# First expert stage: second product in three rounded parts, first product issued three blocks ahead, and the work beside it in another order

## The reference

```python
def _L0_ffn_ref(x, Wg, W1, W2, W3):                    # E = 8 experts, F = 256, top 2
    scores = jnp.einsum('bsd,ed->bse', x, Wg)
    topk_scores, topk_idx = jax.lax.top_k(scores, 2)
    topk_probs = jax.nn.softmax(topk_scores, axis=-1)
    h1 = jnp.einsum('bsd,efd->bsef', x, W1)
    h2 = jnp.einsum('bsd,efd->bsef', x, W2)
    hidden = jax.nn.silu(h1) * h2
    expert_out = jnp.einsum('bsef,edf->bsed', hidden, W3)
    onehot = jax.nn.one_hot(topk_idx, scores.shape[-1], dtype=x.dtype)
    gating = jnp.einsum('bsk,bske->bse', topk_probs, onehot)
    return jnp.einsum('bse,bsed->bsd', gating, expert_out)
...
    x = _layernorm(x + _L0_attn_ref(x, ...))           # "front" work: output projection, norm, router
    x = _layernorm(x + _L0_ffn_ref(x, ...))            # experts; "back" work: residual, norm
    x = _layernorm(x + _L1_attn_ref(x, ...))           # "back" work also: q, k, v of this attention
    x = _layernorm(x + _L1_ffn_ref(x, ...))
```

## Time and profile before

| | us |
|---|---|
| median of 3 runs (lowest to highest) | 1793.75 (1791.52 to 1801.08) |
| the profiled execution: its time | 1795.82 |
| its span, first to last instruction | 1794.0 |
| first copy of y in the first expert stage to the last | 407.9 to 757.9 |
| TensorE busy, VectorE busy, ScalarE busy over the span | 92%, 80%, 68% |
| mean granted TensorE clock | 0.965 |

### The profile page before, as it was taken

One profiled execution on the slowest core, in us unless ns is written; L12 is line 12 of the kernel. 1 busy time (PEld: TensorE's weight loads), 2 busy tenths in 40 slices (PEclk: granted clock), 3 DMA queues, 4 the chain that ended last, 5 costly groups with the idle time before them and its releaser, 6 DMA issues.

```text
span 1794.0 us, 33595 instructions
## 1 busy us (share of the span) xinstructions
PE 1642.9 (92%) x11168; PEld 846.0 (47%) x11168; DVE 1443.7 (80%) x2519; ACT 1213.3 (68%) x1843; POOL 107.4 (6%) x187
## 2 busy tenths in 40 slices
PE   5899999699999999869999999999999978888887
PEld 3333333266556656524444444444444436665565
DVE  3779999867777777688999999999999926778777
ACT  3889999643444444318888888888888876655555
POOL 1000000001101010210000000000000000001000
PEclk9899999899999999969999999999999988999999
DMA  7572323101101111220111111111111010000000
GB/s 219 152 223 82 98 83 94 51 14 49 36 23 38 48 48 35 96 65 30 42 36 36 36 36 35 41 35 36 36 43 49 21 40 14 20 20 19 26 18 12
DMA packets 63717, 95.92 MB, mean 53 GB/s; under 512 B 22512, under 2 KB 31600, under 8 KB 62976
## 3 DMA queue, kind: packets, MB, share of 16 engines
q1 hardware_dynamic: 63616, 94.56, 17.4%
HBM read 51.01 MB, written 43.52 MB: 53 GB/s over the span
## 4 chain that ended last, share of the span: by engine, by line
PE 70%; DVE 11%; issue 8%; ACT 5%; SPq 3%; DMA 2%; POOL 1%; DVEq 0%; ACTq 0%; POOLq 0%
PE full_o L717 15%; PE hid_pair L1014 11%; PE max_pair L688 11%; PE score L702 7%; PE causal_o L449 5%; PE bank L1103 5%; PE triple L433 5%; PE bank L1023 2%; DVE negmax_h L802 2%; PE bank L1044 2%; PE bank L1115 2%; ACT cprobs L477 1%; ACT o_sb L776 1%; SPq L591 1%; PE bank L1069 1%
## 5 line engine op out<-in xcount | busy, mean ns | idle before, releaser
L802 DVE TENSOR_REDUCE negmax_h<-max_pair 128x2 f32<-128x1024 f32 x512 | 620.8, 1222 | 40.0 <-PE max_pair L688 38.6
L768 ACT ACTIVATE probs<-score 128x512 f32<-128x512 f32 x1024 | 556.0, 597 | 118.8 <-PE score L702 70.6
L717 PE MATMUL full_o<-probs,v_st 128*32 128x256 f32 x4096 | 327.7, 392 | 16.3 <-ACT o_sb L776 16.3
L477 ACT ACTIVATE cprobs<-triple 128x1536 f32<-128x1536 f32 x192 | 265.6, 1454 | 21.2 <-PE triple L433 18.4
L688 PE MATMUL max_pair<-k_st,q_st 64*128 64x512 f32 x1024 | 262.1, 509 | 9.9 <-DVE negmax_h L802 9.8
L702 PE MATMUL score<-q_st,k_st 64*128 64x512 f32 x1024 | 224.5, 405 | 0.3 <-ACT probs L768 0.3
L688 PEld LDWEIGHTS max_pair<-k_st,q_st 64*128 64x128 f32 x1024 | 98.0, 188 | 222.5 <-issue 187.3
L1014 PE MATMUL hid_pair<-x_hi,w_hi 128*128 128x512 f32 x384 | 182.4, 475 | 6.9 <-ACT act_s L1216 6.8
L1211 ACT ACTIVATE act_s<-hid_pair 128x512 f32<-128x512 f32 x128 | 76.4, 597 | 158.3 <-PE hid_pair L1014 158.3
L507 DVE TENSOR_SCALAR cprobs<-cprobs 128x1536 f32<-128x1536 f32 (+6 forms) x272 | 163.4, 624 | 0.4 <-ACT cprobs L477 0.4
L717 PEld LDWEIGHTS full_o<-probs,v_st 128*32 128x32 f32 x4096 | 82.0, 108 | 169.1 <-issue 87.0
(11 more groups left out here) (136 smaller groups left out, 1696.0 us busy)
## 6 DMA issues: line engine op xcount, KB each, us to landing
o_scr<-o_sb SPq DMA_DIRECT2D x64, 256.0 KB, 2.1
k_st<-k_scr SPq DMA_DIRECT2D x64, 128.0 KB, 2.9
q_st<-q_scr SPq DMA_DIRECT2D x128, 64.0 KB, 2.4
q_st<-q_scr SPq DMA_DIRECT2D x16, 512.0 KB
k_st<-k_scr SPq DMA_DIRECT2D x64, 104.0 KB
q_scr<-qk_hi SPq DMA_DIRECT2D x24, 256.0 KB, 2.9
k_scr<-qk_hi SPq DMA_DIRECT2D x24, 256.0 KB, 3.4
q_scr<-qk_lo SPq DMA_DIRECT2D x16, 256.0 KB, 3.0
```

The lines of the kernel that those rows point to most:

```text
L477: nc.scalar.activation(cprobs[n % CP][:, :, :], triple[n % 2][:, :, :], ACT.Exp, scale=SCALE).then_inc(L.exp_done, 1)
L717: last = nc.tensor.matmul(full_o[SLOT * j:SLOT * (j + 1), cols], v_st[p][:, kt, j, :], probs[s % NP][:, j, cols], start=(kt == 0 and part ...
L768: nc.scalar.activation(probs[s % NP][:, L.HEADS[j], :], sbank[L.score_bank(e)][:, :], ACT.Exp, scale=SCALE).then_inc(L.exp_done, 1)
L802: nc.vector.tensor_reduce(negmax_h[:, qt // TPC, half, heads[0]:heads[1] + 1:2, qt % TPC], ring[slot][:, :, :], AXX, ALU.max, negate=True) ...
```

## The change

The second product takes three F32R matmuls. ScalarE rounds `hid` to `hid0_hi` (`act_upper`), VectorE subtracts for `hid0_lo` (`dve_lower`), both three buffers deep, and `w3` is split once ahead of chunk 0. The hidden product goes three blocks ahead, the engines' beside work comes two blocks late, and the plan puts the front ahead of the back. The copy of y moves into block 2 of the next chunk. The `Fori` loops over chunks 1 to 6 are written out, in both layers. Zeroing is cut in eight pieces, GpSimd's work is interleaved by step, and the loads of `x` share four semaphores.

```diff
-LATE = (0, 2)
+LATE = (2, 2)
+HB0 = 3
...
-    BESIDE_BACK = {4: (0, 1), 5: (2, 3), 6: (4, 5)}
+    BESIDE_BACK = {6: (0, 1), 7: (2, 3), 8: (4, 5)}
+    CLEARS = 2
...
+            w3_hi = overlay.enter_context(nc.sbuf_tensor("w3_hi", [P, NH, P], F32R))
+            w3_lo = overlay.enter_context(nc.sbuf_tensor("w3_lo", [P, NH, P], F32R))
...
-        for pl, steps in ((plan[0], (1, 3, 4, 5, 6, 7, 8, 9, 10, 11, None, 12, 13, 14)),
+        for pl, steps in ((plan[0], (2, 4, 6, 7, 8, 9, 1, 1, 3, 4, None, 5, 7, 12)),
...
-        h_banks, h_lead = [2, 3], [1, 3]
+        h_banks, h_lead = [2, 3], [3, 3]
+        w_splits = [3, 5]
...
+        FIRST_ROWS = {SPC - 3: 0, SPC - 1: 1}
+
+        def rows_at(n, layer):
+
+            per = SPC // n_exp[layer]
+            if layer == 0:
+                e = (n + 3) // per if n % per == 1 else E0
+            else:
+                e = n // per if n % per == per - 2 else E1
+            return e if e < n_exp[layer] else None
...
                 if n == pl.x2_turn:
                     pe.wait_ge(st.norm2, back + 1)
+                    if front is not None:
+                        pe.wait_ge(st.gate_pre, front + 1)
                     pe_turn_tiles(bank[2], x_out).then_inc(st.xt2_turned, 1)
...
-            pe.wait_ge(st.hid_ready, c * SPC + n + 1)
-            nc.tensor.matmul(bank[0][:, :], w3[:, n, :], hid[n % 2][:, :], start=(n == 0),
-                             stop=(n == SPC - 1)).then_inc(st.y_done, 1)
+            q = c * SPC + n
+            pe.wait_ge(st.lo_ready, q + 1)
+            hi, lo = hid0_hi[q % HB0], hid0_lo[q % HB0]
+            for a, (w, x) in enumerate(((w3_hi, hi), (w3_lo, hi), (w3_hi, lo))):
+                last = nc.tensor.matmul(bank[0][:, :], w[:, n, :], x[:, :], start=(n == 0 and a == 0),
+                                        stop=(n == SPC - 1 and a == 2))
+            last.then_inc(st.y_done, 1)
...
-            with pe.Fori(0, B - 1) as u:
+            for u in range(B - 1):
...
+        def act_upper(act, st, q):
+
+            act.wait_ge(st.hid_ready, q + 1)
+            wait_used(act, st.y_done, q - HB0 + 1)
+            nc.scalar.activation(hid0_hi[q % HB0][:, :], hid[q % 2][:, :], ACT.Copy).then_inc(st.hi_ready, 1)
...
         def act_chunk(act, st, c, par, back, front, layer):
             for n in range(SPC):
+                if layer == 0 and n == LATE[0] and back is not None:
+                    act_save_y(act, st, back)
                 act.wait_ge(st.h_ready, c * SPC + n + 1)
                 wait_used(act, st.hid_ready, c * SPC + n - 1)
                 if layer == 0:
                     nc.scalar.activation(act_s[n % 2][:, :], hbank[n % 2], ACT.Silu).then_inc(st.s_done, 1)
+                    if c * SPC + n > 0:
+                        act_upper(act, st, c * SPC + n - 1)
...
+                if layer == 0 and n == plan[0].x_turn:
+                    act.wait_ge(w_lower, 2)
+                    nc.scalar.activation(w3_hi[:, :, :], w3[:, :, :], ACT.Copy).then_inc(w_upper, 1)
...
+        def dve_lower(dve, st, q):
+
+            dve.wait_ge(st.hi_ready, q + 1)
+            wait_used(dve, st.y_done, q - HB0 + 1)
+            nc.vector.tensor_tensor(hid0_lo[q % HB0][:, :], hid[q % 2][:, :], hid0_hi[q % HB0][:, :].bitcast(F32),
+                                    ALU.subtract).then_inc(st.lo_ready, 1)
...
                     nc.vector.tensor_tensor(hid[n % 2][:, :], act_s[n % 2][:, :], lin_u[n % 2][:, :],
                                             ALU.mult).then_inc(st.hid_ready, 1)
+                    if c * SPC + n > 0:
+                        dve_lower(dve, st, c * SPC + n - 1)
...
+                if layer == 0 and n == plan[0].g_turn:
+                    dve.wait_ge(w_upper, w_splits[0])
+                    nc.vector.tensor_tensor(w3_lo[:, :, :], w3[:, :, :], w3_hi[:, :, :].bitcast(F32),
+                                            ALU.subtract).then_inc(w_lower, 1)
...
                 if c == 2 * B - 1:
+                    sp_first_full(sp, layers[1])
+                    sp.wait_ge(st.y_done, 2 * B * SPC)
                     sp.dma_start(w_raw[0][:, :], d["we1"]).then_inc(raw_loaded[0], 16)
                     sp.dma_start(w_raw[1][:, :], d["we2"].rearrange("p n c -> p (n c)")).then_inc(raw_loaded[1], 16)
-                    sp_first_full(sp, layers[1])
```

More of the change, by code:

```diff
@@ L311, in build_program @@
             x_out = osb("x_out", [P, TPC, D])
+            hid0_hi = [osb(f"hid0_hi{i}", [P, CH], F32R) for i in range(HB0)]
+            hid0_lo = [osb(f"hid0_lo{i}", [P, CH], F32R) for i in range(HB0)]
         q_scr0 = nc.dram_tensor("q_scr0", [B, P, 2, T], F32, kind="Internal").ap()
@@ L336, in build_program @@
         layers = [Causal(sem), Full(sem)]
+        X_GROUPS = [(0,), (1,), (2, 3), (4, 5, 6, 7)]
+        x_group = [k for k, cs in enumerate(X_GROUPS) for c in cs]
         class Stage:
@@ L352, in __init__ @@
                 if n == 0:
-                    self.x_in = [sem(f"st0_x_in{c}") for c in range(2 * B)]
+                    self.x_in = [sem(f"st0_x_in{k}") for k in range(len(X_GROUPS))]
                     self.pair_stored = [sem(f"st0_pair_stored{p}") for p in range(2)]
@@ L1056, in pe_beside @@
                     if layer == 0 and back is not None:
-                        pe.wait_ge(st.v_saved, back + 1)
+                        wait_used(pe, st.v_saved, back)
                     for t in range(TPC):
@@ L1185, in act_beside @@
                     nc.scalar.activation(gate_t[:, :], bank[3][0:2 * E0, :], ACT.Copy).then_inc(st.gate_t, 1)
-                if n == SPC - 1 and layer == 0:
-                    act_gate_rows(act, st, front, 0, layer)
+                if layer == 0 and n in FIRST_ROWS:
+                    act_gate_rows(act, st, front, FIRST_ROWS[n], layer)
         def act_gate_rows(act, st, c, e, layer):
@@ L1235, in act_end @@
                         nc.scalar.activation(w_hi[k][:, :], w_raw[k][:, :], ACT.Copy).then_inc(w_upper, 1)
+                if layer == 0 and n == plan[0].x_turn:
+                    act.wait_ge(w_lower, 2)
+                    nc.scalar.activation(w3_hi[:, :, :], w3[:, :, :], ACT.Copy).then_inc(w_upper, 1)
             act_chunk(act, st, 0, 0, None, 1, layer)
-            with act.Fori(0, B - 1) as u:
+            for u in range(B - 1):
                 act_chunk(act, st, 2 * u + 1, 1, 2 * u, 2 * u + 2, layer)
@@ L1449, in dve_end @@
             dve_chunk(dve, st, 0, 0, None, 1, layer)
-            with dve.Fori(0, B - 1) as u:
+            for u in range(B - 1):
                 dve_chunk(dve, st, 2 * u + 1, 1, 2 * u, 2 * u + 2, layer)
@@ L1469, in pool_rstd, with pool_beside, pool_end0, pool_end1 @@
             nc.gpsimd.tensor_tensor(rstd[:, k, :], rstd[:, k, :], mhalf[:, :], ALU.pow).then_inc(sig, 1)
-        def pool_back(pool, pc, st, c, layer):
-            pool_rstd(pool, pc, st.stats2, st.rstd2, 1, c + 1)
-            if layer == 0:
-                for a in range(2):
-                    pool.wait_ge(st.rot_done, 2 * c + a + 1)
+        def pool_beside(pool, pc, st, n, back, front):
+            pl = plan[0]
+            if front is not None and n == pl.o_proj:
+                pool_rstd(pool, pc, st.stats, st.rstd, 0, front + 1)
+            if back is not None and n == pl.y_turn:
+                pool_rstd(pool, pc, st.stats2, st.rstd2, 1, back + 1)
+            for a, at in enumerate((pl.q, pl.k)):
+                if back is not None and n == at:
+                    pool.wait_ge(st.rot_done, 2 * back + a + 1)
                     nc.gpsimd.tensor_tensor(rot[2 * a][:, :], rot[2 * a][:, :], rot[2 * a + 1][:, :],
                                             ALU.add).then_inc(st.rot_sum, 1)
-        def pool_end(pool, st, layer):
+        def pool_end0(pool, st):
+            pc = Chain(pool, st.pool_chain)
+            for n in range(SPC):
+                pool_beside(pool, pc, st, n, None, 0)
+            for c in range(2 * B):
+                back, front = c - 1 if c > 0 else None, c + 1 if c < 2 * B - 1 else None
+                for n in range(SPC):
+                    if n >= LATE[0]:
+                        pool_beside(pool, pc, st, n - LATE[0], back, front)
+                    if c == 2 * B - 1 and n >= SPC - 2:
+                        for k in range(layers[1].CLEARS):
+                            pool_clear_full(pool, layers[1], layers[1].CLEARS * (n - SPC + 2) + k)
+            for k in range(2 * layers[1].CLEARS, CPB * HG):
+                pool_clear_full(pool, layers[1], k)
+            for n in range(SPC):
+                pool_beside(pool, pc, st, n, 2 * B - 1, None)
+        def pool_end1(pool, st):
             pc = Chain(pool, st.pool_chain)
```

61 lines of the change are left out of this document (33 added, 28 removed).

## The result

The changed kernel takes 1813.03 us (median of 6 runs, 1810.73 to 1822.06) where the kernel before takes 1793.68 in the same rounds (6 runs): ratio 1.0104, 95% interval 1.0073 to 1.0136. It is slower by 1.0%, about 19 us, against the +7 forecast, and its median lies 1 us above the forecast's range of 1776 to 1812.

The account below looks back on a forecast made before the run. TensorE alone was taken to bound the kernel before, a cycle through TensorE and VectorE the new one. Six chunks +17.4, chunk 0 +1.0, chunk 7 -6.0 and loops -5.4 made +7.0 on 1793.75: 1800.8 us, range 1776 to 1812.

Parts of the forecast that it names:

- The cycle through both engines: Steady first-stage chunks: waits in program order through TensorE and VectorE sum to 53.7 us for 50.8, +17.4 over six.
- The collision with GpSimd: First rotary sum of 1.27 us starting during weigh: VectorE delayed by 0.3, bounds 0 and 1.27.
- Chunk 7: Last chunk of the first expert stage, which has no front: 39.2 us for 45.2, -6.0.
- step 2: VectorE from hid 9 to the end of the second rotary pair: 7.43 us, plus 0.3 for GpSimd's rotary sum.
- The ends: Terms outside the steady chunks: first chunk +1.0 us, last chunk -6.0, loop back edges of the second expert stage -5.4.
- the written-out loops: Second expert stage, chunks 1 to 6: without back edges -5.4 us, bounds 0 and -5.6.
- I take 2.7 twice: Two back edges in the second expert stage, each a 2.78 us VectorE gap, disappear: -5.4 us.
- The third rival: Writing out the chunk loops does nothing, so the -5.4 falls away: 1806 us, chance 0.13.
- the forecast's term for the moved waits: Chunk 0 of the first expert stage: moved rows and waits together give -0.4 us.
- The second rival: GpSimd's rotary sum blocks VectorE's weigh in full, 0.85 us, 0.55 more than taken: 1804 us, chance 0.17.
- The first rival: First-stage plan keeps its covers, VectorE running ahead: 1765 us, or 1778 with half the waits kept; chance 0.22 at 1778.

Follow-up runs that it names:

- the second execution: Unmodified changed kernel run and profiled once more, in the rounds of the fillers experiment: 1812.97 us, ratio 1.0114 against the kernel before.
- loops alone: Kernel before with only the chunk loops of both expert stages written out on TensorE, ScalarE and VectorE: 1789.50 us, ratio 0.9990.
- the best variant: Changed kernel with weigh, x2_turn and y-copy repairs, x_turn and its followers one step later, copy of v on ScalarE: 1784.73 us, ratio 0.9946.

## Why the prediction was wrong

**The mechanism held.** The cycle through both engines, by its own steps, in the chunk shown above:

1. End of top 2 (488.90 + 0.17) to `hid` 9 at 494.00: 4.93 for 4.76. The two loads of 1.28 stand back to back with the exponential between them, as the forecast took them from the earlier trace rows; from the first load to silu (490.50 to 493.31) are 2.81 again. The drain of 1.38 per load of the Trainium skill (ScalarE: Activation LUTs, "What ACT_TABLE_LOAD costs") is not seen here either.
2. `hid` 9 to the end of the second rotary pair (501.49 + 0.68): 8.17 for 7.73. **The collision with GpSimd was sized at 0.3 and is 0.88**: 1.04 for 0.16.
3. From there to the copy of y at 520.91: 18.7 for 18.45.
4. Copy of y (466.85) to `hid` 2 at 468.02: 1.2 for 1.4.
5. `hid` 2 to the end of top 2: 21.05 for 21.4.

Sum 54.1 for 53.7. Moving one edge at a time took 1.4, 1.5 and 1.0 away, for 2.1, 1.3 and 1.4 expected. That the sum is off by only 0.4 is partly luck: the five steps are off by +0.2, +0.4, +0.3, -0.2 and -0.3. Chunk 7 came as worked out, 39.1 for 39.2. The waits stand where the text put them: `ot`, `xs`, `lead`, the rotary results.

**The steps that failed** are terms of the sum that were sized too small or too favourably, nearly all on the same side: GpSimd's collision in step 2, chunk 0 in "The ends", and the written-out loops. By the second execution's +18.7 less 7.0, 11.7 are missing:

- **Up to the first copy of y**: +5.5 for +1.0, the largest of them. 1.4 of it is there before the stage starts (the last `causal_o` at 340.67 for 339.26); this start varies, from 337.1 to 343.2 in the sixteen profiles. The second gate row added 1.48 for the 1.4 forecast. The other 2.7 lie between the first hidden product and the first copy of y, where the forecast had -0.3: about 1.4 of them are the clock and 1.3 the change, as the rows below show.
- **The cycle**: +20.7 for +17.4, of which some 2.4 are GpSimd's collision and the small errors above (54.1 for 53.7) and 0.8 the mean of the six, 54.23.
- **Loops written out**: -2.4 for -5.4 in the second execution, -2.5 in the first. The step "I take 2.7 twice" is borne out as far as the two gaps go, which are gone; besides the clock 4.1 are saved, and 1.7 of this went again on more time at the low clock, for which the forecast had no term. The third rival (it does nothing, 1806) was about half right in the size and not in the mechanism; timed alone, the loops can't be told from zero.
- **Between the stages**: +1.0 for 0, within what this stretch varies by (773.0 and 776.1 for the same kernel).

Chunk 7 gives 0.2 back. The window rows from the first hidden product to the first copy of y, of the kernel before and of loops alone:

```profile
360.11:407.87 47.76, 46.88 (x168) 29.38 (x167) 30.08 (x72) 20.65 (x33) 1.27 (x2) 0.97 0.05 13
```
```profile
357.95:408.51 50.56, 49.67 (x168) 31.02 (x167) 30.10 (x72) 20.69 (x32) 1.27 (x2) 0.91 0.04 12
```

The same 168 matmuls, 2.8 apart. The stage begins at the low clock behind waits of 5 us; it stayed low for some 3 us of the first row and some 9 of the second. The changed kernel's second execution takes 50.45, its first 49.80. Less the missing clock, estimated as above, these are 46.2 and 46.0 before, and 47.4 and 47.8 after. So the forecast took the one chunk 0 that it had for the kernel's, and that was a short one; but the change also costs 1.3 to 1.9 there. TensorE waits 1.9 to 2.2 in this stretch of the changed kernel (`ot`, `xs`, `lin_u`) where it waited 0.9 before, and the forecast's term for the moved waits was -0.4.

The second rival (GpSimd's sum blocks weigh in full) had the mechanism and the duration: 0.85 forecast, 0.88 measured, 1804 as its time. The exclusive lock that the Trainium skill states (SBUF — State Buffer, "Who interferes with whom") agrees with the rotary sums, down to an operation of four elements a partition. It does not fit GpSimd's power of 1.04 us on 128x4, which also has two inputs: `hid`, begun 0.1 into it, keeps its 0.69 (474.90 above), as in every chunk. The first rival (covers kept) fell, though its idea returns in the run with the plain product and four buffers.

The range ended at 1812, at "the third rival with a us of error per chunk". It had no room for several small misses adding up, which is what happened: half of the loops' gain gone, the second rival's lock, and a start sized from one short execution. The chance of 0.36 for slower was too low on the same ground. Of the unknown costs the loops (0 to -5.6, taken at -5.4) and the collision (0 to 1.27, taken at 0.3) both stood near their favourable ends, and chunk 0 was given -0.4 for moved waits with no row behind it.

**Not settled**: why the clock falls in one chunk and not in the next behind the same waits, why a fall lasts 3 to 4 us or 10, why the stage begins with 3 us or 9 at the low level, and what exactly bounds the best variant at 50.3. The kernel before has one profile only, so its stretches are single readings.

## What to carry to other kernels

When a change relieves the full engine by loading the next one, don't compare two sums: follow the new order through both engines once round, wait by wait; it gave 53.7 for 54.1, where the larger of the two sums was 47.5. The repairs then come from that list of edges: an operation moved into another's wait, a wait put on the reading of a buffer rather than on the end of the whole step, a copy moved behind the operation that others await. They turned +1.0% into -0.5% with the same product. Ask of a fall of the clock whether the engine has a wait behind it: here 3 to 4 us at half clock cost nothing with one, and 1.2 to 1.9 without. And before taking a ring of buffers out with the operation that filled it, ask what it decoupled: two buffers for four cost 15 to 18 us a chunk.

## What the hardware showed unexpectedly

One GpSimd addition of 1.27 us stretched each VectorE operation with both inputs in SBUF that started during it: 1.04 for 0.16 at 128x4, 1.27 or 1.35 for 0.69 at 128x512; `lin_u`, which reads one input from PSUM, keeps its 0.68 beside the same sum, and `hid` keeps its 0.69 beside GpSimd's power of 1.04. In the steady chunks of the changed kernel the granted clock fell to the 1.2 GHz level only behind TensorE's longer waits (2.1 to 2.5 for `xs`, 1.9 for `lead`, 1.5 for `v`), though not behind each of them, and matmuls with no purpose in those waits kept it at 1.00 through seven chunks, without making the kernel faster that the timed runs could tell. In the kernel before, the same stage, with waits of about 1 a chunk, held 1.00 throughout.
